# An attention and expert-mixture kernel on one core: the third unit of a group weighed ahead of the odd step's two gate sums

## The reference

```python
x = x + xattn(layernorm(x), ctx)           # q, k, v with biases; softmax over 375 keys
h_in = layernorm(x)
router = softmax(h_in @ w_router)           # 8 experts
gates  = softmax(h_in @ w_gating / 0.1)
g = einsum('bsh,ehf->ebsf', h_in, w_gate)   # 256 -> 1024 for each expert
u = einsum('bsh,ehf->ebsf', h_in, w_up)
expert_out = einsum('ebsf,efh->ebsh', silu(g) * u, w_down)
cw = router * gates;  cw = cw / (sum(cw) + 1e-9)
x = x + einsum('ebsh,bse->bsh', expert_out, cw)
```

## Time and profile before

| | us |
|---|---|
| median of three runs | 987.1 (982.05 to 990.15) |
| the profiled execution, its own time | 986.0 |
| its span, first to last instruction | 984.2 |
| PE busy | 977.5 (99%) |
| PEld busy | 892.3 (91%) |
| DVE busy | 732.9 (74%) |
| ACT busy | 484.7 (49%) |
| POOL busy | 779.2 (79%) |

### The profile page before, as it was taken

One profiled execution on the slowest core, in us unless ns is written; L12 is line 12 of the kernel. 1 busy time (PEld: TensorE's weight loads), 2 busy tenths in 40 slices (PEclk: granted clock), 3 DMA queues, 4 the chain that ended last, 5 costly groups with the idle time before them and its releaser, 6 DMA issues.

```text
span 984.2 us, 14884 instructions
## 1 busy us (share of the span) xinstructions
PE 977.5 (99%) x5188; PEld 892.3 (91%) x5188; DVE 732.9 (74%) x1278; ACT 484.7 (49%) x858; POOL 779.2 (79%) x619
## 2 busy tenths in 40 slices
PE   8999999999999999999999999999999999999998
PEld 7999899999899989989989989999999899989998
DVE  7987347777777777778777777777877777777786
ACT  6988554444535444544445444444445444444441
POOL 5699976767878788878888787888889887879752
PEclk9999999999999999999999999999999999999999
DMA  9341221411010110011100110011101100111202
GB/s 232 89 136 52 67 71 51 130 61 41 22 43 22 41 60 24 22 62 41 43 22 23 45 58 22 23 61 41 44 22 46 57 23 22 43 41 41 75 1 75
DMA packets 43426, 51.59 MB, mean 52 GB/s; under 512 B 2980, under 2 KB 39304, under 8 KB 43352
## 3 DMA queue, kind: packets, MB, share of 16 engines
q1 hardware_dynamic: 43344, 50.64, 16.9%
q10 hardware_dynamic: 8, 0.00, 0.0%
HBM read 45.07 MB, written 5.56 MB: 51 GB/s over the span
## 4 chain that ended last, share of the span: by engine, by line
PE 99%; ACT 1%; issue 0%; DVE 0%; DVEq 0%
PE ps L318 95%; PE ps L1711 1%; PE ps L1739 0%; PE ps L1812 0%; PE ps L1700 0%; PE ps L1756 0%; PE ps L1782 0%; PE ps L1945 0%; ACT arena L808 0%; ACT early L744 0%; PE ps L1807 0%; PE ps L1657 0%; DVE arena L322 0%; ACT arena L775 0%; ACT arena L763 0%
## 5 line engine op out<-in xcount | busy, mean ns | idle before, releaser
L318 PE MATMUL ps<-arena 128*128 128x448 f32 (+5 forms) x2112 | 397.1, 338 | 1.3 <-DVE arena L322 1.1
L318 PEld LDWEIGHTS ps<-arena 128*128 128x128 f32 (+2 forms) x2112 | 350.6, 186 | 24.6 <-DVE arena L1193 1.1
L566 POOL TENSOR_TENSOR arena<-shared,arena 128x448 fp32r<-128x448 f32 x196 | 247.3, 1276 | 142.8 <-ACT arena L930 139.7
L318 PE MATMUL ps<-xc_hi,w_hi 128*128 128x448 f32 x904 | 337.0, 373 | 0.2
L318 PE MATMUL ps<-xc_hi,w_lo 128*128 128x448 f32 x904 | 330.8, 366 | 0.0
L318 PE MATMUL ps<-xc_lo,w_hi 128*128 128x448 f32 x904 | 330.6, 366 | 0.0
L318 PEld LDWEIGHTS ps<-xc_hi,w_hi 128*128 128x128 f32 x904 | 169.7, 188 | 28.9 <-DVE shared L1323 10.5
L318 PEld LDWEIGHTS ps<-xc_hi,w_lo 128*128 128x128 f32 x904 | 169.8, 188 | 14.6
L318 PEld LDWEIGHTS ps<-xc_lo,w_hi 128*128 128x128 f32 x904 | 170.0, 188 | 13.0
L923 ACT ACTIVATE shared<-shared 128x448 f32<-128x448 f32 x180 | 101.4, 580 | 161.6 <-DVE shared L1306 88.8
L1300 DVE TENSOR_TENSOR shared<-ps,shared 128x448 f32<-128x448 f32 x60 | 37.5, 625 | 139.7 <-PE ps L318 139.7
(11 more groups left out here) (164 smaller groups left out, 1144.4 us busy)
## 6 DMA issues: line engine op xcount, KB each, us to landing
early<-in_L_ffn_w_down SPq DMA_DIRECT2D x16, 512.0 KB, 3.8
xf<-cw_dram SPq DMA_DIRECT2D x16, 448.0 KB, 4.7
shared<-in_ctx SPq DMA_DIRECT2D x16, 336.0 KB
w_raw<-in_L_ffn_w_gate SPq DMA_DIRECT2D x17, 256.0 KB, 2.8
w_raw<-in_L_ffn_w_up SPq DMA_DIRECT2D x17, 256.0 KB, 3.3
early<-in_L_ffn_w_gate SPq DMA_DIRECT2D x15, 256.0 KB, 2.7
early<-in_L_ffn_w_up SPq DMA_DIRECT2D x15, 256.0 KB, 3.2
x_dram<-xsacc SPq DMA_DIRECT2D x8, 224.0 KB, 3.0
```

Of the source, the lines that this page charges most:

```text
L318: ins = nc.tensor.matmul(dst, w, m, start=first and i == 0, stop=last and i == len(passes) - 1, skip_group_check=onto)
L566: nc.gpsimd.tensor_tensor(h[:, 1, j, at:at + TC], tile, h[:, 0, j, at:at + TC].bitcast(fp32), ALU.subtract).then_inc(hid_lo_done, 1)
```

## The change

In the odd step of a turned group, VectorE's `weigh(g, 2)` is written ahead of `gate_u3_c22(n)` instead of behind it. For the other groups `add_rows` stays where it was.

```diff
@@ -1609,10 +1609,10 @@
                 up_u2(n)
                 if n == QUADS - 2:
                     add_back(0, 1)
-                gate_u3_c22(n)
                 if odd and g in TURNED:
                     weigh(g, 2)
-                elif odd:
+                gate_u3_c22(n)
+                if odd and g not in TURNED:
                     add_rows(g, 2, ps_r[2])
                     add_rows(g, 3, ps_r[3])
                 if n == QUADS - 2:
```

## The result

The changed kernel takes 973.46 us (median of four executions, 973.08 to 974.55) against 985.28 us before (982.05 to 990.15): a ratio of 0.988, 95% interval 0.983 to 0.992, so it is 1.2% faster. I had forecast 987.3 us, no change. 973 us is the time of the case that the prediction called "fast throughout" (972.7 us, chance 0.36).

What follows compares the result with a forecast made beforehand. PE was taken as the bound, its time lost in late weight loads. From 986.0 us: +1.5 for slow spacing over 27 periods, -0.3 for the 28th stall, +0.1 behind it, giving 987.3 us; range 971 to 990 us.

Steps and rivals of the forecast that it cites:

- fast throughout: Case: 28 stalls gone, whole loop at 0.2026 us per matmul; 972.7 us, chance 0.36.
- The stall and what causes it: In 28 odd steps, PE's weight loads wait for late up sums on VectorE; about 0.34 us each, 0.27 at slow spacing.
- GpSimd's 0.25 us of cover: GpSimd's first addition frees the buffer of weigh(g,2) before its unit is done; forecast 0.26 us ahead.
- Step n = 4: Step already having the new order, its load unmarked by any wait; taken as evidence that the stall would cost nothing.
- The two spacings: Between stalls, 128x448 matmuls start 0.2026 or 0.2066 us apart, changing only where a wait disturbed the stream.
- the last draw at 185 us: Weight load's wait for GpSimd's L560 at 185.24 us, said to set the whole loop's spacing once the stalls are gone.
- slow 0.45: Likeliest case, chance 0.45: 28 stalls gone, whole loop at 0.2066 us per matmul; 987.3 us.
- so was 166.40: Second ground for the slow case: the lone wait at 166.40 us also left slow spacing, 0.206 us.
- case M: Spacing drawn again on the way through the loop, fast and slow mix as before; 977.0 us, chance 0.12.
- (a): Rival: another wait behind the two sums keeps loads late, so PE gains nothing; 986.0 us, chance 0.04.
- (b): Rival: weigh(g,2) waits for GpSimd's addition and holds the gate sums; slower, near 1017 us if two additions late; chance 0.03.
- The margin of 0.09 us: In the odd step, up's last load possible at 500.97 us against 501.06 due; called thin.

Runs made afterwards that it cites:

- e3: Changed kernel with weigh(g,2) moved behind both the gate and up sums in all 28 odd steps; median 973.82 us, its profiled execution 987.72 us.
- e2: Changed kernel with weigh(g,2) back behind the gate sums in eight odd steps; median 978.7 us, ratio 0.992 to the kernel before.
- e5: Changed kernel with PE running unit 0 of group 2 behind up_4_3 instead of ahead, in step n = 6 alone; median 972.58 us.
- e6: The changed kernel run again without edits; executions 972.57, 973.24, 973.75 and 987.94 us.
- e4: Changed kernel with weigh(g,2) between the two gate sums in all 28 odd steps; median 982.0 us, ratio 0.995 to the kernel before.
- e1: Changed kernel with weigh(g,2) back behind the gate sums in group 15's odd step only; executions 973.4, 973.64, 973.76 and 980.92 us.

## Why the prediction was wrong, point by point

- **The stall and what causes it: right.** 28 times 0.34 or 0.27 us, from the up sums (e3). In step n = 29 the details were right too: the lag of 0.40 us, the 0.60 us left over, GpSimd's 0.25 us of cover, loads in step behind the up sums. Step n = 4 was the right witness.
- **Reading weight loads instead of matmul busy time: right.** Matmul idle time is the same 1.3 us before and after. The Trainium skill ("Perfetto Trace Analysis", section "Identifying the Most-Contended Engine") calls the busy share of the matmuls a poor measure of how near TensorE is to its limit; the traces agree, with 99% before and after.
- **The two spacings, held through the loop, and the last draw at 185 us: right**, shown by e2, e3, e5 and the one piece of 3669 matmuls. The times of both cases were right within 1 us: 972.7 against 973.46, and 987.3 against 987.72 (e3) and 987.94 (e6).
- **The choice between the cases: wrong, and this is the step that failed.** The prediction gave slow 0.45 and fast 0.36 because "the disturbance that sets it was slow here", and so added +1.5 us for a loop at 0.2066 us where the measured loop ran at 0.2026 (its own term for that: -12.7 us). That was one execution's outcome, taken for a property of the kernel. In the 12 executions told of above the same wait left slow spacing twice, so fast was the likely case by about 5 to 1. The second ground, "so was 166.40", falls as well: that slow spacing ended at the 256-column matmuls of 168.36 us, without a wait, and behind the same wait ten of the eleven kept traces are fast. "The spacing changes only where a wait has disturbed the stream" was therefore wrong outside the loop. Could the odds have been known? Only in part. 20 of the 28 stalls of the profile before left fast spacing, but nine of these were met at slow spacing; of those met at fast spacing, as the wait at 185 us was, 11 left fast and 8 slow. That favours fast a little, not 5 to 1, and e4 shows that another kind of wait can have other odds. That the first four executions of the changed kernel were all fast is partly luck: at 2 in 12 it happens about every second time.
- **The range, 971 to 990 us, held the time**, because it was drawn to reach both cases; the chance of faster by over 1%, 0.42, was too low for the same reason as above.
- **A small slip in a sum:** case M counts the 28 stalls as 20 of 0.34 and 8 of 0.27 us; the stall at 201 us was met at slow spacing too, so it is 19 and 9, and 0.07 us less. It changes nothing.
- **"Spacing drawn again on the way" (M)**: did not happen in the 3668 intervals of the loop, neither at fast spacing (changed kernel) nor at slow (e3).
- **Rivals (a) and (b)**: neither happened. The margin of 0.09 us for the last load sufficed in all 28 steps, and PE waited for L1300 and L1302 in none.

## What to carry to other kernels

When an engine is busy for 99% and still paces the kernel, look for stalls in the starts of its instructions (here the weight loads), not in its idle time; and give an operation that nobody waits for a place outside the pairs of sums that the bound engine waits for. Where one profile shows the outcome of something that can come out otherwise in the next execution, do not take that outcome for the kernel's own: count the outcomes of the same kind in the same situation, and where there is only one, run more executions before choosing. A kernel whose executions scatter by 0.8% may have such a thing in it. Once stalls are few, look also at those ahead of a long undisturbed loop, since each of them can set the pace of the whole loop.

## What the runs showed of the hardware that I had not expected

Back-to-back float32r matmuls of 448 columns with their weight loads run at 0.2026 or 0.2066 us from start to start, at the same granted clock, and kept to one of them for 3668 intervals in which no load had to wait (743.84 and 758.52 us for the same 3669 matmuls, 2.0% apart). Waits of 0.40 us left the slow one in one trace (e3) and the fast one in another (e1). Twelve matmuls of 256 columns brought the slow one back to fast without a wait (168.36 us, kernel before). That waits of one kind (e4), met at fast spacing, left it fast 28 times of 28, and those of another 11 times of 19, I had not expected either, and it is not explained; nor is it that all 10 stalls met at slow spacing left fast.
